# A gated cross-attention block with routed experts: fourth quad's transposes moved behind the next scores, banks reassigned, values behind the queries

## What is computed

```
x   = x + tanh(g0) * Attention(layernorm(x), ctx)      # 16 heads of 16, causal softmax
x   = x + tanh(g1) * Experts(layernorm(x))             # top 1 of 14 experts, 256 -> 512 -> 256, gelu
Attention: q = h Wq + bq, k = ctx Wk + bk, v = ctx Wv + bv
           softmax(q k^T / 4 + mask) v, then the dense matrix Wd and its bias
Experts:   expert = argmax(h Wr), weight = softmax(h Wr)[expert]
           weight * (gelu(h W1[expert] + b1) W2[expert] + b2)
```

## Time and profile before

| | us |
|---|---|
| median of 3 runs | 534.56 |
| the runs | 533.37, 534.73, 534.56 |
| the profiled execution | 533.33 |
| its span, first to last instruction | 531.40 |
| mean granted TensorE clock in it | 0.965 |

### The profile page before, as it was taken

The page is one execution under the profiler, slowest core; times in us unless marked ns, Lnnn a source line. Parts: engine busy times, 40 slices in busy tenths (PEclk is TensorE's granted clock), DMA queues, the critical chain, the costliest instruction groups (busy, mean ns, idle before and its releaser), DMA issues.

```text
span 531.4 us, 16942 instructions
## 1 busy us (share of the span) xinstructions
PE 478.5 (90%) x4893; PEld 414.7 (78%) x4894; DVE 331.9 (62%) x1046; ACT 324.7 (61%) x1459; POOL 272.4 (51%) x502
## 2 busy tenths in 40 slices
PE   2799999999999999999999973199999999999991
PEld 2578888888888888788888853089999999999880
DVE  1568798988888888888889866024343433434330
ACT  1589899898889889798898960033334243334320
POOL 5343536456456555645655434336555655555621
PEclk9999999999999999999999986589999999999997
DMA  7154564122121111212110101499889888887800
GB/s 248 45 182 134 168 192 146 48 57 65 51 69 50 66 43 50 69 49 69 40 59 20 43 21 41 90 339 292 259 269 290 280 267 271 289 262 235 297 2 1
DMA packets 37333, 72.65 MB, mean 137 GB/s; under 512 B 12585, under 2 KB 20911, under 8 KB 37296
## 3 DMA queue, kind: packets, MB, share of 16 engines
q10 hardware_dynamic: 7056, 29.72, 17.6%
q1 hardware_dynamic: 23184, 25.68, 15.8%
q0 software_dynamic: 7056, 16.79, 9.4%
HBM read 58.79 MB, written 15.07 MB: 139 GB/s over the span
## 4 chain that ended last, share of the span: by engine, by line
PE 44%; ACT 27%; DVE 11%; issue 9%; DMA 5%; POOL 2%; SPq 1%; DVEq 1%; ACTq 0%; another core or an unknown queue 0%; POOLq 0%
ACT arena L538 25%; PE bank L1047 14%; PE bank L1057 14%; PE bank L900 3%; DVE negmax L652 3%; PE bank L878 2%; PE bank L892 2%; DMA arena<-token_rows,arena 2%; PE bank L1034 2%; DMA arena<-x 2%; PE bank L976 1%; ACT arena L568 1%; DVE stats L785 1%; PE bank L908 1%; PE bank L987 1%
## 5 line engine op out<-in xcount | busy, mean ns | idle before, releaser
L538 ACT ACTIVATE arena<-bank,negmax 128x128 f32<-128x128 f32 x512 | 182.4, 405 | 40.3 <-DVE negmax L652 40.3
L538 ACT ACTIVATION_READ_ACCUMULATOR arena<-bank,negmax 128x1 f32 x512 | 124.8, 244 | 0.0
L608 ACT ACTIVATE arena<-bank,w_ring 128x128 f32<-128x128 f32 x180 | 51.5, 369 | 84.9 <-issue 44.6
L1047 PE MATMUL bank<-arena,w_ring 128*128 128x128 f32 x720 | 89.5, 278 | 0.6 <-issue 0.6
L652 DVE TENSOR_REDUCE negmax<-bank 128x4 f32<-128x512 f32 x128 | 84.1, 679 | 6.1 <-PE bank L892 4.6
L1057 PE MATMUL bank<-W,arena 128*128 x360 | 85.9, 382 | 1.2 <-DVE arena L847 1.0
L1047 PEld LDWEIGHTS bank<-arena,w_ring 128*128 128x128 f32 x720 | 85.6, 195 | 1.0 <-issue 1.0
L900 PE MATMUL bank<-C,arena 128*128 128x128 f32 x512 | 79.9, 280 | 5.5 <-ACT arena L538 4.0
L847 DVE SCALAR_TENSOR_TENSOR arena<-bank,arena 128x256 f32<-128x256 f32 x45 | 21.8, 484 | 100.2 <-PE bank L1057 87.0
L427 POOL TENSOR_TENSOR arena<-arena,C 128x256 f32<-128x256 f32 x64 | 37.9, 612 | 83.6 <-ACT arena L568 83.6
L900 PEld LDWEIGHTS bank<-C,arena 128*128 128x128 f32 x512 | 61.0, 143 | 20.5 <-ACT arena L538 9.1
(11 more groups left out here) (109 smaller groups left out, 744.3 us busy)
## 6 DMA issues: line engine op xcount, KB each, us to landing
w_ring<-w1b ACTq DMA_DIRECT2D x45, 642.0 KB
token_rows<-rows SPq DMA_DIRECT2D x32, 256.0 KB, 2.2
W<-w SPq DMA_DIRECT2D x14, 512.0 KB
arena<-x SPq DMA_DIRECT2D x32, 128.0 KB, 2.1
arena<-ctxt SPq DMA_DIRECT2D x32, 128.0 KB, 2.1
arena<-token_names SPq DMA_DIRECT2D x45, 1.0 KB
arena<-token_rows,arena POOLq DMA_INDIRECT x45
out<-arena POOLq DMA_INDIRECT x45
```

Source lines behind the costliest of these rows:

```text
L538: ins = act.activation(probs[:, q, v, :], bank[q][:, v * P:(v + 1) * P], ACT.Exp, bias=negmax[:, b.par, h:h + 1], accum_out=rsum[:, b.par, ...
L608: ins = act.activation(hid_t[:, k, ch, :], hid_bank[k][:, ch * P:(ch + 1) * P], ACT.Gelu, bias=w_ring[:, k, B1_AT + ch:B1_AT + ch + 1])
L1047: ins = pe.matmul(hid_bank[r][:, f * P:(f + 1) * P], w_ring[:, r, at:at + P], g_xt[:, r, ch, :], start=(ch == 0), stop=(ch == DC - 1))
```

## The change

The copies, transposes and blocks of code move as follows. The transposes of quads 0 and 1 go into the score banks 0 and 1, those of quads 2 and 3 into bank 4. The values are projected into bank 5, behind the transposes of quad 2. The transposes of quad 3 leave the end of the step and go behind the next step's scores; ScalarE's copy of them goes behind its copy of the layer norms. `attend` goes behind the queries. On VectorE the second maximum follows the first at once, the block of line 688 goes behind the query copies, the fourth maximum and the copy of quad 0 behind that, the reciprocal of line 735 behind the first statistics. On ScalarE the copy of quad 2 goes ahead of that of the values. Waits are changed with them.

```diff
@@ -229,2 +229,3 @@
 
+        probs_bank = [bank[0], bank[1], bank[4], bank[4]]
         hid_bank = [bank[k] for k in (0, 1, 2, 6, 7)]
@@ -546,6 +547,4 @@
                     act.activation(probs_t[:, q, :, :].rearrange("p v s -> p (v s)"),
-                                   bank[4 + q % 2][:, :], ACT.Copy).then_inc(probs_t_scalar, 1)
+                                   probs_bank[q][:, :], ACT.Copy).then_inc(probs_t_scalar, 1)
 
-                if c.ok():
-                    transposed_probs(c, 3)
                 if a.ok() or d.ok():
@@ -559,2 +558,4 @@
                                    bank[6][:, lo * P:hi * P], ACT.Copy).then_inc(xh_ready, 1)
+                if c.ok():
+                    transposed_probs(c, 3)
                 if b.ok():
@@ -572,2 +573,3 @@
                     exponentials(3)
+                    transposed_probs(b, 2)
                 if a.ok():
@@ -578,7 +580,5 @@
                         ins = act.activation(values[:, a.slot, e_, :, e_ * DH:(e_ + 1) * DH],
-                                             bank[0][:, e_ * P:(e_ + 1) * P].rearrange("p (h w) -> p h w", h=HG),
+                                             bank[5][:, e_ * P:(e_ + 1) * P].rearrange("p (h w) -> p h w", h=HG),
                                              ACT.Copy)
                     ins.then_inc(v_raw_ready, 1)
-                if b.ok():
-                    transposed_probs(b, 2)
                 if e.ok() and e.par == 1:
@@ -660,3 +660,3 @@
                     dve.tensor_copy(probs_t[:, q, :, :].rearrange("p v s -> p (v s)"),
-                                    bank[4 + q % 2][:, :]).then_inc(probs_t_vector, 1)
+                                    probs_bank[q][:, :]).then_inc(probs_t_vector, 1)
 
@@ -670,2 +670,3 @@
                     maxima(0)
+                    maxima(1)
                 last = c.static and c.n == B - 1
@@ -680,15 +681,3 @@
                 if b.ok():
-                    maxima(1)
                     maxima(2)
-                if c.ok():
-
-                    dve.wait_ge(rinv_t_ready, c.n + 1)
-                    dve.wait_ge(av_done, c.n + 1)
-                    wait(dve, dense_done, c.n)
-                    dve.tensor_tensor(attn_t, bank[7][:, 0:D], rinv_t, ALU.mult).then_inc(attn_ready, 1)
-                if a1.ok():
-                    wait(dve, xh_transposed, a1.n - 1)
-                    normed(a1, xn[:, a1.par, :], x_in[:, a1.slot, :], moments, rstd, rstd_ready, xn_ready)
-                    if a1.static and a1.n == 0:
-                        cast_constants()
                 if mixed:
@@ -707,6 +696,7 @@
                         dve.sem_inc(mixed_ready, 1)
-                if b.ok():
-                    transposed_probs(0)
-                if h.ok() and not (h.static and h.n == B - 1):
-                    normed(h, rows[:, h.slot, 0:D], rows[:, h.slot, D:2 * D], moments2, rstd2, rstd2_ready, h_ready)
+                if a1.ok():
+                    wait(dve, xh_transposed, a1.n - 1)
+                    normed(a1, xn[:, a1.par, :], x_in[:, a1.slot, :], moments, rstd, rstd_ready, xn_ready)
+                    if a1.static and a1.n == 0:
+                        cast_constants()
                 if a2.ok():
@@ -721,4 +711,13 @@
                         fold_gate()
+                if c.ok():
+
+                    dve.wait_ge(rinv_t_ready, c.n + 1)
+                    dve.wait_ge(av_done, c.n + 1)
+                    wait(dve, dense_done, c.n)
+                    dve.tensor_tensor(attn_t, bank[7][:, 0:D], rinv_t, ALU.mult).then_inc(attn_ready, 1)
                 if b.ok():
                     maxima(3)
+                    transposed_probs(0)
+                if h.ok() and not (h.static and h.n == B - 1):
+                    normed(h, rows[:, h.slot, 0:D], rows[:, h.slot, D:2 * D], moments2, rstd2, rstd2_ready, h_ready)
                 if c.ok():
@@ -732,5 +731,2 @@
                     transposed_probs(1)
-                    dve.wait_ge(probs_ready, b.n * 4 + 4)
-                    wait(dve, rinv_rep_ready, b.n)
-                    dve.reciprocal(rinv[:, :], rsum[:, b.par, :]).then_inc(rinv_ready, 1)
                 if f.ok() and f.par == 1:
@@ -785,2 +781,6 @@
                     dve.bn_stats(stats2[:, c.slot, :], rows[:, c.slot, D:2 * D]).then_inc(stats2_done, 1)
+                if b.ok():
+                    dve.wait_ge(probs_ready, b.n * 4 + 4)
+                    wait(dve, rinv_rep_ready, b.n)
+                    dve.reciprocal(rinv[:, :], rsum[:, b.par, :]).then_inc(rinv_ready, 1)
                 if a.ok():
@@ -896,6 +896,6 @@
 
-                def transpose_probs(q):
-                    pe.wait_ge(probs_ready, b.n * 4 + (q + 1))
+                def transpose_probs(n, q):
+                    pe.wait_ge(probs_ready, n.n * 4 + (q + 1))
                     for v in range(HQ):
-                        ins = pe.transpose(bank[4 + q % 2][:, v * P:(v + 1) * P], probs[:, q, v, :], ident)
+                        ins = pe.transpose(probs_bank[q][:, v * P:(v + 1) * P], probs[:, q, v, :], ident)
                     ins.then_inc(probs_transposed, 1)
@@ -922,6 +922,10 @@
                     pe.wait_ge(k_masked_ready, b.n + 1)
-                    pe.wait_ge(v_raw_ready, b.n + 1)
+                    wait(pe, probs_t_vector, b.n * 2)
+                    wait(pe, probs_ready, b.n * 4)
                     scores()
                 if c.ok():
-                    pe.wait_ge(probs_t_scalar, c.n * 2 + 2)
+                    pe.wait_ge(probs_t_scalar, c.n * 2 + 1)
+                    transpose_probs(c, 3)
+                    pe.wait_ge(v_raw_ready, t.n - 2 if a.ok() or b.ok() else B)
+                    wait(pe, mixed_ready, t.n - 4)
                 if e.ok():
@@ -929,3 +933,3 @@
                     pe.wait_ge(xh_ready, t.n - 2)
-                    if not b.ok():
+                    if not c.ok():
                         pe.wait_ge(mixed_ready, t.n - 4)
@@ -953,7 +957,2 @@
                     ins.then_inc(mixed_done, 1)
-                if c.ok():
-
-                    pe.wait_ge(probs_t_vector, c.n * 2 + 2)
-                    wait(pe, x2_ready, c.n)
-                    attend()
                 if a.ok():
@@ -965,4 +964,11 @@
                     queries_keys(0, wq_sb)
+                if c.ok():
+
+                    pe.wait_ge(probs_t_vector, c.n * 2 + 2)
+                    pe.wait_ge(probs_t_scalar, c.n * 2 + 2)
+                    pe.wait_ge(v_raw_ready, c.n + 1)
+                    wait(pe, x2_ready, c.n)
+                    attend()
                 if b.ok():
-                    transpose_probs(0)
+                    transpose_probs(b, 0)
                 if a.ok():
@@ -979,4 +985,5 @@
                 if b.ok():
-                    wait(pe, mixed_ready, t.n - 3)
-                    transpose_probs(1)
+                    transpose_probs(b, 1)
+                    wait(pe, probs_t_scalar, b.n * 2)
+                    transpose_probs(b, 2)
                 if a.ok():
@@ -985,9 +992,7 @@
                         pe.wait_ge(v_w_loaded, 16)
+                    wait(pe, mixed_ready, t.n - 3)
                     for ch in range(DC):
-                        ins = pe.matmul(bank[0][:, 0:D], c_in[:, a.slot, ch, :], wv_sb[:, ch, :],
+                        ins = pe.matmul(bank[5][:, 0:D], c_in[:, a.slot, ch, :], wv_sb[:, ch, :],
                                         start=(ch == 0), stop=(ch == DC - 1))
                     ins.then_inc(v_done, 1)
-                if b.ok():
-                    pe.wait_ge(probs_t_vector, b.n * 2 + 1)
-                    transpose_probs(2)
                 if a1.ok() or h.ok():
@@ -1010,5 +1015,2 @@
                     ins.then_inc(xh_transposed, 1)
-                if b.ok():
-                    pe.wait_ge(probs_t_vector, b.n * 2 + 2)
-                    transpose_probs(3)
```

## The result

| | before | changed |
|---|---|---|
| median of 4 runs, us | 533.96 | 558.48 |
| lowest and highest | 532.85, 534.73 | 557.73, 559.04 |
| the profiled execution | 533.33 | 558.92 |
| its span | 531.40 | 557.1 |

The ratio is 1.046, with a 95% interval of 1.0434 to 1.0487. The change makes the kernel 4.6% slower; the forecast was 560.0.

A forecast was written before the change was run, and what follows sets the result against it. TensorE, busy 63.61 of 64 us at full load, was taken as the bound. Terms of +0.98 us a step (9.23 to 10.21) made +26.7 us over the kernel, against 533.33: 560.0 us, range 553 to 569.

The forecast's parts named there:

- The deciding part: VectorE's multiplication of attention by the reciprocals, now behind the query copies, makes TensorE's dense start 1.22 us later in a step.
- the round trip from keys to dense: TensorE's keys end, VectorE's query copies and multiplication follow, then dense starts at 163.57 instead of 162.35: 1.22 us.
- exposed weights: Dense on TensorE, after its wait, no longer hides its first weights: 0.10 us taken, from 0.1 to 0.15.
- The step: One inner step of TensorE in the attention stage: 9.32 us on average before, 10.25 after, over 27 steps.
- The sum for the inner step: Step taken apart on TensorE: +1.22 + 0.10 − 0.19 − 0.15 = +0.98 us, 9.23 to 10.21.
- the 0.6 us that the second batch's scores were to gain: Early attention steps: the second batch's scores lose the fourth transposes ahead of them, −0.6 us.
- The waits: Expected signs: dense idle about 1.2 us, VectorE 1.5 to 2 ahead of query copies, ScalarE about 2, clock 1.00.
- The reciprocal "is worth nothing": VectorE's reciprocal behind the first statistics removes a wait of about 0.8 us a step, worth nothing as TensorE sets the step.
- the ring through the reciprocal and routing: Last exponentials, VectorE's reciprocal, routing and statistics, next batch's first maximum, exponentials; the reciprocal waits 26.5 us in all.
- The banks "cost 0 to 0.1": New banks for transposes and values add waits only for work long done: cost 0 to 0.1 us, taken as 0.
- The ring rival: Attention stage: if the multiplication ended before the keys, the step would fall to 8.89 us, 522 in all; chance 0.05.
- The second rival: Fourth quad's copy delays exponentials, or statistics the first maximum: 0.3 to 0.5 us in 27 steps, 568 to 574; chance 0.14.

## Why the prediction was right, and where it was not

**The deciding part** was sized right. I had 1.22 us for the round trip from keys to dense, measured 1.19; 0.10 for exposed weights, measured 176.61 − 175.64 = 0.97 against 0.86, so 0.11. Moving the multiplication back, adding the move to the old kernel, and halving what stands ahead of it all moved the time as that mechanism says: −19.9, +30.4, −6.9 us.

**The step** was to be 10.25 us on average. Scores start at 55.99 and 332.53 with 27 steps between, 10.24. The sum for the inner step, 10.21 against 10.19 measured, is right in part by luck, for smaller terms were off both ways. The fourth transposes took a slot of 0.50 instead of my 0.44, as their first weight load starts only together with them, at 169.94; the first transposes took 0.49 instead of 0.43, and the layer norms' transposes 0.53 instead of 0.44, now that the scores follow them. Router and reciprocals' transposes took 0.37 and 0.25 instead of 0.47 and 0.34. That is 0.21 more and 0.19 less. Of the terms outside the inner steps, the 0.6 us that the second batch's scores were to gain came to 1.0 (26.66 instead of 27.70).

**The waits** came mostly as forecast: VectorE idle 1.6 us on average ahead of the query copies (50.1 / 31), the first transposes of a step hardly ever waiting for the exponentials (TensorE waited for them three times in all), the clock at 1.00. ScalarE's idle time ahead of the fourth quad's copy was 1.2 us where I had said about 2.

**The reciprocal "is worth nothing"** was wrong for the kernel before; for the changed kernel no run tests it by itself. In the kernel before, TensorE's 0.19 us of idle time in the step that I took apart led me to treat TensorE as the bound; but steps there are 9.32 on average and only 9.04 of it is work, and the ring through the reciprocal and routing held most of the difference. With the reciprocal moved, steps average 9.14 us and the kernel is 5.6 us shorter.

**The banks "cost 0 to 0.1"** holds for the changed kernel, whose long step covers it, as I had written: there the copy of quad 1 ends 0.4 to 0.9 us before the next scores in the steps at full load. I underrated what comes with a short step. The ring rival promised 522 us once the multiplication is early; it gave 536.6. The term that failed is the copy of quad 1: it was to end 0.7 us ahead of the scores, and in a short step it ended after TensorE was ready, 0.51 us of idle time in the step shown. The norm ahead of it had a slot of 0.65 us instead of 0.32; that stretch alone is 0.33 of the 0.51. The second rival ("a second stall") did not come true in the changed kernel. A second stall showed only once the multiplication was early, and not at the place that I had named.

## To carry to other kernels

When two engines hand work back and forth, look at what an instruction stands *behind* on its queue. In the kernel before, moving a multiplication of 0.41 us whose inputs were ready cost 30 us in all, because it then stood behind a wait for the very matmuls that its consumer follows. Gains from taking a ring apart are seen only once no longer wait covers them, and each wait removed should be followed by a look at which came next: the same move of the norm gave 11.7 us or nothing.

## What the runs showed of the hardware

VectorE's norm, from SBUF to SBUF, took 0.40 us in the kernel before and up to 0.83 in the changed one, where it runs beside GpSimd's masking of the keys:

```profile
166.00 1.19 POOL L428 TENSOR_TENSOR arena<-arena,C 128x256 f32<-128x256 f32 x2 [3.25 <-ACT arena L569]
...
166.50 0.83 DVE L666 TENSOR_SCALAR rows<-rows,moments,rstd 128x256 f32<-128x256 f32 x1
```

It ends at 167.33, shortly after GpSimd's at 167.19. Over the kernel (durations in ns, min/median/max), changed kernel first, then the one with the norm moved:

```profile
L666 DVE TENSOR_SCALAR rows<-rows,moments,rstd x32: 404/670/835, 44.0 to 350.4; 128x256 f32<-128x256 f32 x32
```

```profile
L666 DVE TENSOR_SCALAR rows<-rows,moments,rstd x32: 401/405/414, 40.0 to 349.7; 128x256 f32<-128x256 f32 x32
```

The Trainium skill, page "SBUF — State Buffer", section "SBUF: two separate sides", says that VectorE, in some of its modes, and GpSimd take turns at one pair of ports, and that the later one waits for the other's whole instruction. The rows fit that in the main: the norm ends 0.14 us after GpSimd does, and takes 0.405 us where nothing stands beside it. One thing they don't settle: the norm started 0.07 us before the second of GpSimd's two instructions, at 166.57, and still ended behind it. That it is the ports and not something else was not tried by itself.
